# Cross-attention, projection and expert loop on one core: two program blocks made into one, with work of the second moved into the last attention blocks

## The reference, cut to what matters

```python
def reference(x, ctx_1024, _lenS2, ln_g, ln_b, Wq, bq, Wk, bk, Wv, bv, Wo, bo, gate_w, w1, w2, w3):
    x = x + attention(layernorm(x), ctx_1024, ctx_1024, _lenS2, ...)   # 16 heads of 64, rope, masked keys, @ Wo + bo
    x = x + ffn(layernorm(x), gate_w, w1, w2, w3)                      # 8 experts, top 2, silu(x w1) * (x w3) @ w2
    return x
# x is [1, 2048, 256], ctx_1024 is [1, 1601, 256], everything float32; d_ff is 512
```

## Time and profile before

| | us |
|---|---|
| median of 3 runs (1208.84 to 1212.22) | 1210.13 |
| the profiled execution, span | 1211.3 |
| PE busy | 1070.4 (88%) |
| DVE busy | 979.4 (81%) |
| ACT busy | 731.4 (60%) |
| POOL busy | 644.6 (53%) |
| last pair of heads, up to PE's last matmul of the attention | about 817 to 898.4 |
| PE idle between the attention and the projection | 898.4 to 909.6 |
| projection and routing | 909.6 to 1004 |
| expert loop | 1004 to 1211 |

### The profile page before, as it was taken

How to read it: one execution, slowest core, us unless ns; L and a number is a source line. 1 busy time by engine, 2 the same in 40 slices (tenths; PEclk the granted TensorE clock), 3 DMA queues, 4 the chain that set the end, 5 groups by cost and what they waited for, 6 DMA issues and landing times. The chain is left out here.

```text
span 1211.3 us, 32849 instructions
## 1 busy us (share of the span) xinstructions
PE 1070.4 (88%) x12843; PEld 709.2 (59%) x13030; DVE 979.4 (81%) x1769; ACT 731.4 (60%) x1298; POOL 644.6 (53%) x457
## 2 busy tenths in 40 slices
PE   1468999999999999999999999999969958999995
PEld 1334566566656656656665665666648944566663
DVE  5878999999999999999999999999944674455552
ACT  2635666666666666666666666766644643455552
POOL 1045764674585477467448647733449554333333
PEclk9679999999999999999999999999988979999998
DMA  8034242332423324143242433317526522333330
GB/s 280 0 97 115 79 107 63 98 91 69 107 79 97 96 81 104 51 122 84 77 99 76 110 79 90 79 38 224 207 99 231 174 84 84 57 52 57 54 60 12
DMA packets 104445, 117.01 MB, mean 97 GB/s; under 512 B 47389, under 2 KB 86494, under 8 KB 103006
## 3 DMA queue, kind: packets, MB, share of 16 engines
q1 hardware_dynamic: 91214, 99.74, 29.5%
q0 software_dynamic: 7152, 8.43, 4.2%
q10 hardware_dynamic: 5920, 6.65, 2.0%
HBM read 39.46 MB, written 36.87 MB: 63 GB/s over the span
## 5 line engine op out<-in xcount | busy, mean ns | idle before, releaser
L829 ACT ACTIVATE prob<-sc,key_bias 128x512 f32<-128x512 f32 x640 | 405.3, 684 | 149.2 <-PE sc L683 145.1
L962 DVE TENSOR_REDUCE part_max<-mx 128x1 f32<-128x427 f32 x768 | 417.3, 590 | 35.8 <-PE mx L700 35.8
L1106 POOL TENSOR_TENSOR prob_lo<-prob 128x1024 bf16<-128x1024 f32 x128 | 242.5, 1894 | 229.4 <-ACT prob L829 229.3
L974 DVE TENSOR_TENSOR prob_lo<-prob 128x1024 bf16<-128x1024 f32 x192 | 278.2, 1449 | 9.8 <-ACT prob L829 6.2
L727 PE MATMUL pv<-VV,prob 128*128 128x65 bf16 x2560 | 267.9, 193 | 3.7 <-POOL prob_lo L1106 3.5
L729 PE MATMUL pv<-VV,prob_lo 128*128 128x65 bf16 x2560 | 269.3, 195 | 0.0
L728 PE MATMUL pv<-VV,prob 128*128 128x64 bf16 x2560 | 268.0, 193 | 0.0
L727 PEld LDWEIGHTS pv<-VV,prob 128*128 128x128 bf16 x2560 | 239.8, 99 | 38.8 <-POOL prob_lo L1106 7.3
L728 PEld LDWEIGHTS pv<-VV,prob 128*128 128x128 bf16 x2560 | 237.2, 97 | 26.4
L683 PE MATMUL sc<-Q,K 65*128 65x512 bf16 x640 | 243.6, 381 | 10.3 <-issue 4.0
L700 PE MATMUL mx<-K,Q 128*128 128x427 bf16 x768 | 236.6, 349 | 9.7 <-DVE part_max L962 5.1
(11 more groups left out here) (208 smaller groups left out, 1470.8 us busy)
## 6 DMA issues: line engine op xcount, KB each, us to landing
expert_inputs<-zeros SPq DMA_DIRECT2D x129, 129.0 KB, 2.8
we<-in_w_exp SPq DMA_DIRECT2D x8, 1536.0 KB, 7.9
Q<-we SPq DMA_DIRECT2D x45, 256.0 KB, 3.8
attention_out<-o_out SPq DMA_DIRECT2D x64, 128.0 KB, 2.0
o_in<-attention_out SPq DMA_DIRECT2D x16, 512.0 KB, 3.7
q32s<-q SPq DMA_DIRECT2D x122, 64.0 KB, 2.0
K<-we SPq DMA_DIRECT2D x48, 160.0 KB, 3.9
VV<-next_v SPq DMA_DIRECT2D x16, 322.5 KB, 4.0
```

The costliest lines, as they stand in the source:

```text
L829: act.activation(prob[:, s % PRING, j, :], sc[n % 2][:], ACT.Exp, bias=key_bias[:, t:t + 1], scale=HD ** -0.5).then_inc(exp_done, 1)
L962: dve.tensor_reduce(part_max[:, b_ % 2, qt, h:h + 1], mx[:, pl.part_banks(qt, h)[0]:pl.part_banks(qt, h)[-1] + 1, 0:pl.width], mybir.AxisL ...
L974: dve.tensor_tensor(prob_lo[:, s % PRING, 0:g, :], prob[:, s % PRING, 0:g, :], hi_half(prob[:, s % PRING, 0:g, :])[:, :, 1::2], ALU.subtra ...
L1106: pool.tensor_tensor(prob_lo[:, s % PRING, 0:g, :], prob[:, s % PRING, 0:g, :], hi_half(prob[:, s % PRING, 0:g, :])[:, :, 1::2], ALU.subtr ...
```

## The change

The two blocks become one, so that there is no common stop between them; SP's wait for the last stored rows moves to the load that needs them. The steps of the projection are made functions (`turn_o`, `high_o`, `low_o`, `load_o`, `load_first_x`, `split_half`), which `attend` calls in the last pair, and the second part leaves out what has been done by then:

- SP loads the first four tiles into `o_in` in slot 2 of block 6, behind the expert loads.
- ACT issues the loads of x's first chunk and of `gate` in slot 2 of block 6.
- PE turns tiles 0 and 1 in the two closing slots behind block 7 (slots 40 and 41 of the pair), ahead of the last two `times_v`; ACT makes their `OH` and DVE their `OL` there.
- POOL splits one half of the experts' weights (`split_half`) behind its `low` of slot 3 in each of blocks 1 to 7, seven of the 16.
- The buffers of the attention are allocated in another order, and those of the projection for the whole kernel, so that nothing overlaps that is live.

The diff without the changed indentation and allocations:

```diff
+        attention = attend(nc, sem, maker, locals())
+        mixing = experts(nc, sem, maker(whole), locals())
+        with nc.Block() as block:
+            @block.tensor
+            def _(pe):
+                attention["tensor"](pe, mixing["turn_o"])
+                mixing["tensor"](pe)
...
 # attend, PE
+                    if last and s >= BLOCKS * pl.groups:
+                        if s == BLOCKS * pl.groups:
+                            pe.wait_ge(part_read, PAIRS * BLOCKS * pl.block_parts + pl.part_slots)
+                            pe.wait_ge(v_lo_made, PAIRS * pl.v_units)
+                        turn_o(pe, s - BLOCKS * pl.groups)
                     if s >= LAG:
                         times_v(p, s - LAG)
...
+                pe.wait_ge(exp_done, PAIRS * BLOCKS * pl.kt + 2)
 # attend, ACT
+                    if last and s == (BLOCKS - 2) * pl.groups + LAG:
+                        act.wait_ge(qk_lo_made, PAIRS * QK_UNITS)
+                        for a in range(2):
+                            act.wait_ge(v_loaded[a], 16 * PAIRS)
+                        act.wait_ge(pv_done, PRING + pl.groups * (PAIRS * BLOCKS - CH))
+                        load_first_x(act)
+                    if last and s >= BLOCKS * pl.groups:
+                        high_o(act, s - BLOCKS * pl.groups)
 # attend, DVE
+                    if last and s >= BLOCKS * pl.groups:
+                        if s == BLOCKS * pl.groups:
+                            dve.wait_ge(qk_lo_made, PAIRS * QK_UNITS)
+                        low_o(dve, s - BLOCKS * pl.groups)
 # attend, POOL
                         if m in pl.pool_groups and not (last and s >= BLOCKS * pl.groups):
                             low(p, s)
+                        if last and m == pl.pool_groups[1] and i >= 1:
+                            split_half(pool, i - 1)
 # attend, SP
+                            if s // pl.groups == BLOCKS - 2:
+                                for t in range(QT):
+                                    load_o(sp, t)
...
-                    for i in range(2):
-                        sp.wait_ge(o_stored[i], 16 + 16 * PAIRS * BLOCKS // 2)
 # project_and_mix
+    def load_o(sp, t):
+        c = t // QT
+        if t % QT == 0:
+            sp.wait_ge(o_stored[c % 2], 16 + 16 * ((PAIRS - 1) * BLOCKS // 2 + (CH + c) // 2 + 1))
         if t >= OB:
             sp.wait_ge(ot_ready, t - OB + 1)
         sp.dma_start(o_in[:, t % OB, :], o_dram[t * P:(t + 1) * P, :]).then_inc(o_loaded[t % OB], 16)
...
+    def split_half(pool, n):
+        if n % 2 == 0:
+            pool.wait_ge(we_loaded[n // 2], 16)
+        pool.tensor_tensor(half(we_lo, n), half(we, n), half(we_hi, n), ALU.subtract).then_inc(we_split, 1)
...
-                for n in range(2 * E):
+        for n in range(BLOCKS - 1, 2 * E):
...
 # in each engine's loop over the steps
-                    if t < ST:
+            if LAG <= t < ST:
```

More of the change, by code:

```diff
@@ new lines, in experts @@
+    logits = sb("logits", [P, ST, E])
+    g8 = [sb(f"g8_{i}", [P, QT, E]) for i in range(3)]
+    picks = sb("picks", [P, 2, QT, E])
+    pick = [picks[:, k] for k in range(2)]
+    picked_slots = sb("picked_slots", [P, 2, QT, E])
+    top = sb("top", [P, 4, QT])
+    ew = sb("ew", [P, 2, 4, QT])
+    chosen = sb("chosen", [P, ST, E], BF16)
+    filled = sb("filled", [P, E, ST])
+    tiles = sb("tiles", [P, 4, E])
+    tri = sb("tri", [P, E, E])
+    slot_of = sb("slot_of", [P, QT, E])
+    slot_f = sb("slot_f", [P, 2, QT])
@@ new lines, in project_and_mix @@
+    o_stored = have["o_stored"]
+    sb, pb = made
+    wp = [pb(f"wp{i}", [P, 512]) for i in range(2)]
+    yt = pb("yt", [P, 4, P])
+    gp = pb("gp", [P, 512])
+    ot = [pb(f"ot{i}", [P, 2, 4, P]) for i in range(2)]
+    o_loaded = [sem(f"o_loaded{i}") for i in range(OB)]
+    x_in_loaded = [sem(f"x_in_loaded{c}") for c in range(CH)]
+    gate_loaded = sem("gate_loaded")
+    ids_made, shift_made = sem("ids_made"), sem("shift2_made")
+    ot_ready, oh_made, ol_made = sem("ot_ready"), sem("oh_made"), sem("ol_made")
@@ new lines, in sync, with place_of, fetch, load @@
+    def sync(sp):
+        for t in range(QT, ST):
+            load_o(sp, t)
+        for c in range(CH):
+            sp.wait_ge(x1_made, QT * (c + 1))
+            sp.dma_start(out[0, c * QC:(c + 1) * QC, :].rearrange("(t p) d -> p t d", p=P),
+                         x1[:, c * QT:(c + 1) * QT, :]).then_inc(x1_stored, 16)
+        def place_of(i, q=0):
+            row = sp.value_load(tile_row[0:1, bass.ds(q * TURN + i, 1)])
+            placed = sp.value_load(scatters[0:1, bass.ds(q * TURN + i, 1)], min_val=1, max_val=2)
+            return row, placed
+        def fetch(i, row, placed):
+            sp.wait_ge(rows_placed, placed)
+            sp.dma_start(x_in[:, i % TURN, :], x_slots[bass.ds(row, P), :]).then_inc(x_tile[i % TURN], 16)
+        def load(i, q=0):
+            need(sp, xt_ready, q, TURN, i - TURN + 1)
+            sp.wait_ge(y_stored[i % TURN], 16 * (i // TURN))
+            sp.sem_inc(load_turn, 1)
+            fetch(i, *place_of(i, q))
+        def turn(q, tiles_, last):
+            for j in tiles_:
+                if not last or j + TURN < tiles_.stop:
+                    load(j + TURN, q)
+        sp.sem_inc(rows_placed, 1)
+        sp.wait_ge(tables_made, 2)
+        sp.sem_inc(load_turn, 1)
+        first = place_of(0)
+        for c in range(CH):
+            sp.wait_ge(scattered_low[c], 16 * QT)
+        fetch(0, *first)
+        for i in range(1, TURN):
+            fetch(i, *place_of(i))
+        load(TURN)
+        body(turn, sp)
```

2310 lines of the change are left out of this document (1134 added, 1176 removed).

## The result

The changed kernel takes 1223.44 us (median of 5 runs, 1215.42 to 1223.95), the kernel before, timed beside it, 1211.31. The ratio is 1.0096, with a 95% interval of 1.0077 to 1.0116: slower by 1.0%. The forecast was 1216.5, with a range of 1206.5 to 1222. Its direction was right, its size was not, and the median lies 1.4 above the range.

The account below looks back on a forecast made before the run. PE and DVE were taken as both full in the last pair, with PE idle 11.17 at the seam. -15.2 + 0.35 + 18.0 + 1.8 + 1.5 = +6.4 gave 1217.8 against the span, 1216.5 against the median; range 1206.5 to 1222.

Parts of the forecast that it names:

- The seam: Between attention and projection: early tiles let PE turn tile 2 at 903.6 instead of 918.83, a gain of 15.2 us.
- the 0.6 of turning tile 1: In the attention's closing slots: turning tile 1 puts 0.6 of its 0.9 us on PE's path, bounds 0 and 0.9.
- The jump: At the end of the attention: PE's jump over the other program copies costs 1.9 us, bounds 0 and 3.9.
- ACT's 0.35: In block 6: ACT's two early load issues ahead of its row copy lose 0.35 us, bounds 0 and 0.7.
- The conflicts: Blocks 1 to 5: POOL's split delays DVE's `low` in slots 4 and 0, 3.6 us per block, 18.0 in all.
- (A): Stretched blocks: only the first conflict, in slot 4, counts, 2.2 us a block; time 1208, chance 0.22.
- (B): In the attention: the splits hide in POOL's gap and only the seam counts; time 1195, chance 0.11.
- (D): At the seam: another wait, such as on the last stored rows, holds PE as before; time 1230, chance 0.02.
- The clock: Stretched blocks: PE's waits of about 2.1 us let its clock fall; one fall net, 1.5 us, bounds 0 and 7.
- rival (C): At the seam: less gain, through a 3.9 us jump, late tile 4 or a clock fall; time 1221.5, chance 0.15.
- All steps behind keep their distances: Behind tile 2: later steps shift with it unchanged, as PE is gapless there; tile 2 to first expert fetch within 1.
- Making seven splits earlier buys nothing there: In the projection: POOL is no limit, its first scatter coming after 11.41 us idle, so early splits gain nothing.

Follow-up runs that it names:

- no_splits: Changed kernel with the attention's split calls left out and all 16 splits made in the projection; 1209.77 us, 0.9991 of the kernel before.
- filler: Changed kernel with 8 extra 512-column matmuls on PE at slot 2 of blocks 2 to 6 in the last pair; 1217.87 us, 1.0059 of the kernel before.
- one_split: Changed kernel with only one split in the attention, in block 3, and the other 15 in the projection; 1211.19 us, 1.0006 of the kernel before.
- narrow: Changed kernel with each of the seven attention splits cut to 768 of 1536 columns, the rest made in the projection; 1207.34 us, 0.9928 of the kernel before.
- paused_seven: Changed kernel, one split in block 7, the others in the projection; POOL waits after 13 for the first routing, last three in pieces; 1200.64 us, 0.9884 of before.
- paused_one_copy: Changed kernel, all splits in the projection, POOL waiting after 12 for the first routing, last four in pieces, one attention copy; 1200.35 us, 0.9881 of before.

## Why the prediction was right and wrong

- **The seam**: from the attention's last matmul to tile 2, -15.8 forecast (the -15.2 without the 0.6 of turning tile 1, which lies ahead), -14.8 measured. The jump took 2.9 instead of 1.9, within its bounds of 0 and 3.9. The 0.6 for turning tile 1 was right, ACT's 0.35 was not: no_splits ends the attention 1.2 later than before, of which 0.6 is there when the last pair begins (ACT's copies at 816.82 and 816.24) and 0.6 comes with the turnings. Across ACT's issues in block 6 the copies are 9.15 apart, before 9.14. The Trainium skill, "Advanced Engine Details and Errata", section "Control Flow Timing", has about 51 ns for a branch; the runs speak for its "Runtime: NRT & Kernel Launch", section "Instruction fetch mechanics", a wait for the fetch behind the branch, as the idle time goes away with the copies that are jumped over.
- **The conflicts**: right in kind, place and size. `low` was forecast at 3.4 and 2.6 and took 3.3 and 2.7. A block was forecast at 14.5, and is that where the clock stays up (filler: 14.08 to 14.57). The attention without the clock's part was forecast to grow by 18.0, 1.8, 0.35 and 0.6, that is 20.75; filler measured 19.0: four blocks lost 3.1 to 3.7 each where five were counted, as the first split came too late for the first conflict, and the last two lost 4.6 together instead of 2.75. Rivals (A) and (B) are out, and (D), as no wait for stored rows stands at the seam.
- **The clock**: this is the step that failed. "I take one of them net of cover, 1.5; bounds 0 and 7 (four)". It was 7.6 by the difference to filler. The forecast had PE waiting 2.1 at once in each stretched block, and the earlier trace rows with a fall behind 2.27, and yet took one fall for five blocks. Nothing supported one: there was no row of a PE wait of 2 in the attention after which the clock stayed. After has four such waits (1.98 to 2.19) and a fall behind each. The price of a fall was about right (up to 1.7 forecast, 1.9 measured), the count was wrong, and one_split shows that a single wait is enough. With 7.6 in the place of 1.5 the sum is +12.5 and the time 1222.6. That this comes within 1 of the measured 1223.4 is luck: the traces have +10.3, since the rest of the attention (-1.75), the projection (-3.6), the expert loop (+2.0) and the seam (+1.0) were off as well, and the base was off by 3.0 the other way.
- **The clock at the seam** (rival (C)): in after it did not fall, in seven of the experiments it did. The price forecast for it, 2, was about right (1.7); whether it comes was not to be seen from before.
- **"All steps behind keep their distances"**: wrong by -3.6 and +2.0, which partly cancel. Up to the first routing's result the distance is the same (33.6). Behind it about 2 of the 3.6 is the common stop that the trace of before has at 973 and that of after has not, so it belongs to the two executions as much as to the change. The rest, and the expert loop's 2.0, have no single cause in the traces.
- **"Making seven splits earlier buys nothing there"**: wrong, and the most instructive error, though it does not explain the miss. The forecast asked only whether POOL's *end* was late for its scatters, and found 11.41 of slack. It did not ask whom the splits would stand beside once the projection starts 15 earlier. Before, the routing's first subtraction started 0.5 behind the end of the splits: that was the slack that counted. no_splits shows it: without the early splits the change ends at no gain. The same exclusion that it priced in the attention sat in the projection too, on operations of 0.19.

## What to carry to other kernels

Before moving work of GpSimd into an idle gap, list the two-input SBUF operations that VectorE has there, and price each at what is left of GpSimd's operation when it starts, however short it is; do the same for the place from which the work is taken, and for all that shifts with it. Where that makes TensorE wait about 2 us, count a fall of the clock for each such wait, not one for all: here eight useless matmuls in each such wait won 0.4%. And halve the moved operation (narrow), or leave the work where it was and let GpSimd wait out VectorE's critical group: with one semaphore, six of the seven splits back in the projection, one in a covered place and the last three in pieces (paused_seven), 1.0% slower became 1.2% faster.

## What the runs showed of the hardware

- POOL's unspaced pieces of 0.6 kept one DVE operation out for 13.10 us, although 22 of them ended meanwhile; with a semaphore wait between them the delay was at most 0.5. The Trainium skill, "SBUF — State Buffer", section "Who interferes with whom", has the holder keep the pair to the end of its instruction. By that, as read here, the wait would end after one piece; the measurement decides, and it can last until POOL has no piece left.
- A memset on POOL (2.81 us) delayed DVE's two-input subtraction by nothing.
- The jump over three unused copies of the attention cost PE 2.7 to 3.3 us of idle time; with the copies left out PE's next matmul started 0.29 behind the last (paused_one_copy).
- A stop of 4.4 us of PE, ACT and DVE at once, during eight scatters of POOL in a row, in three of the twelve experiments, unexplained. Before shows one of 1.6 to 2.1 at four scatters.
